# Summing the head scores of the odd tiles on TensorE, and spacing out GpSimd's products

## The chip, the cores and the metric

The kernel runs on one core of a Trainium2 chip. The metric is the device time of one execution in microseconds (us), and a version is judged by the median over its runs. A core has TensorE (PE in the profile, its weight loads PEld), VectorE (DVE), ScalarE (ACT) and GpSimd (POOL), and SyncE (SP), which here issues DMAs. They work side by side and wait for one another by semaphores. Each engine takes its own instructions strictly in the order in which they are written.

## The reference, cut to what matters

The reference is a stack of four blocks over 2 x 1024 tokens of width 128. Each block is a layer norm, an attention or mixing branch `s`, a gating feed-forward branch `g`, and `x = x + s * g`. The change touches the third one, whose attention runs over the 16 heads of one token and not over tokens:

```python
qkv = jnp.einsum('bnm,fm->bnf', x, Wqkv)          # 384 per token: q, k, v of 16 heads x 8
scores = jnp.einsum('bnhd,bngd->bnhg', q, k) / SCALE   # 16 x 16 per token, a sum over d = 8
attn = jax.nn.softmax(scores, axis=-1)
out = jnp.einsum('bnhg,bngd->bnhd', attn, v)
return jnp.einsum('bni,mi->bnm', out.reshape(b, n, -1), Wproj) + bproj
```

Beside it runs that block's feed-forward: 8 matrices, of which each position takes one, chosen by a position table.

## The kernel before

The 2048 tokens are cut into 16 tiles of 128. In the heads' attention a token lies on a partition, and one tile passes through these steps (generator `tile(i)`, one in each engine's program; the two tile buffers are taken in turn, `k = i % 2`):

1. TensorE projects the tile to q, k, v (`qkv`, a PSUM bank of 384 columns); ScalarE copies k and v to SBUF.
2. VectorE multiplies q by k for all pairs of heads: 16 x 16 x 8 = 2048 products per partition into `pr1[k]`. The sum index d, of length 8, runs innermost.
3. VectorE sums each 8 of them (`red(s, p1, ADD)`, 2048 read, 256 written into `sc2[k]`) and takes each head's negated maximum (`mx`, 256 read).
4. GpSimd adds the maximum (256 elements, "shifted"), ScalarE takes the exponential.
5. GpSimd multiplies with v in four instructions of 512 elements, the quarters, into `pr2[k]`; VectorE meanwhile sums the exponentials and takes the reciprocal.
6. VectorE sums the 2048 products of step 5 to 128 (`ot2[k]`, in the array `osb`), GpSimd scales them, TensorE turns the tile, ScalarE copies it out.

`pr1`, `pr2`, `sc2` and the q, k, v copies are pieces of one large SBUF array `ar`, so the profile names them all `ar`; `ps` is PSUM. Helpers record the instructions: L235 is every matmul, L238 a transpose by TensorE, L241 a tensor_tensor, L246 a tensor_scalar, L249 a scalar_tensor_tensor, L254 a reduce, L257 a copy, L278 an activation.

The program has three parts. `ORDER_A` and `ORDER_C` are tables: for each engine a string of step names, in which each name advances that step's generator by one `yield`. Between them stands the token attention of the first block, with steps woven in by slot (`LANES_B`). `ORDER_C` holds the second block's experts (`xturn`, `up`, `hturn`, `down` with numbers 2 and 3), its recurrence (`rec`), the heads' attention (`tile.0` to `tile.15`), the third block's feed-forward (`ffn2`: TensorE spreads a choice over a bank, VectorE multiplies it with the tokens into `psum_sb`, TensorE multiplies by the weights, eight times for each of four groups), the gathers of expert outputs (`gather`: GpSimd fetches rows to `gT` and `acc_sb`, VectorE adds them) and the fourth block. PSUM banks 4, 6 and 7 are handed out in turn in this part, and a matmul first waits until its bank has been emptied.

Of the kernel before, what the change touches and what calls it, by code (L numbers as in the profile page):

```python
# [37 lines left out]
for _name, _n in (("wqkvp", 512), ("wq", 128), ("wk", 128), ("wv", 128), ("bw", 128), ("cw", 128), ("wg1", 8),  # L38
# [45 lines left out]
    "vector": (  # L84
# [225 lines left out]

def rows_sem(q, i):
    return f"rows_in{i}" if q < 5 else f"last_rows_in{i}"


class Marks:

# [103 lines left out]
def _program(nc, A, out, ctx):  # L420
# [652 lines left out]
    def vector_program(dve):  # L1073
# [331 lines left out]
        def tile(i):  # L1405
# [18 lines left out]
            if i >= 2:  # L1424
                dve.wait_ge(*at(f"tile{k}_pool", i - 2, "av"))
# [1105 lines left out]
```

## Time and profile before

| what | value |
| --- | --- |
| median of 3 runs (lowest, highest) | 1131.12 us (1123.92, 1132.36) |
| the profiled execution | 1131.41 us, its span 1129.5 us |
| granted TensorE clock, mean over the span | 0.949 |
| busy PE / DVE / ACT / POOL | 1015.3 / 840.9 / 553.1 / 720.6 us |

The span runs from the first to the last instruction; 1.9 us of the execution lie around it. A busy share is an average over stages with different limits, so it is read by stretch below. Granted clock 1.00 is 2.4 GHz, and a stretch below 1.00 is a mix with time at 1.2 GHz. A TensorE matmul of 4-byte numbers appears as two records.

### The profile page before, as it was taken

To read this page: it belongs to the slowest core of one execution; us is meant where nothing else is said; L and a number is where in the kernel's file an instruction comes from. 1 tells how busy PE (TensorE), PEld (TensorE's weight loads), DVE (VectorE), ACT (ScalarE), POOL (GpSimd) and SP (SyncE) were. 2 spreads that over 40 slices of the span, in tenths; PEclk is the share of its full clock that TensorE was granted. 3 is DMA by queue.
4 is the path that set the end of the run, shared out by engine and by line. 5 is a ranking of instruction groups with operands and counts; after the bars stand their busy time and mean duration, and the time that the engine had idled before them with its cause. 6 is when DMAs were issued, how large, how long until landed. Compare 5 with 4: busy or idle time off the path is not lost.

```text
span 1129.5 us, 15337 instructions
## 1 busy us (share of the span) xinstructions
PE 1015.3 (90%) x4930; PEld 426.4 (38%) x4930; DVE 840.9 (74%) x1343; ACT 553.1 (49%) x911; POOL 720.6 (64%) x571
## 2 busy tenths in 40 slices
PE   5899989999999999999989986799957785789998
PEld 3356542222222222222212212567635322347675
DVE  6955768778788879787878525874799989997434
ACT  2564455656566665565556653443444111145353
POOL 5650527899987778997879993042476846861412
PEclk9999999999999999999999988899988786799999
DMA  9363612121111101212010112212200400101322
GB/s 325 102 197 99 181 49 69 29 60 30 33 39 36 35 14 48 60 58 63 20 32 23 37 29 64 90 62 75 80 10 19 182 15 19 47 24 39 97 65 71
DMA packets 84274, 74.19 MB, mean 66 GB/s; under 512 B 21612, under 2 KB 70124, under 8 KB 83300
## 3 DMA queue, kind: packets, MB, share of 16 engines
q1 hardware_dynamic: 70756, 62.45, 17.6%
q0 software_dynamic: 5120, 10.50, 3.2%
q10 hardware_dynamic: 8320, 0.26, 0.3%
q8 instruction: 42, 0.69, 0.3%
q14 instruction: 36, 0.29, 0.1%
HBM read 47.94 MB, written 24.77 MB: 64 GB/s over the span
## 4 chain that ended last, share of the span: by engine, by line
PE 62%; DVE 15%; POOL 11%; issue 4%; ACT 4%; ACTq 1%; DMA 1%; SPq 0%; POOLq 0%; DVEq 0%
PE ps L235 56%; POOL psum_sb L241 8%; PE ps L238 6%; DVE ar L241 4%; DVE ar L254 3%; ACT ar L278 2%; DVE small L254 2%; POOL xsort L295 1%; ACTq L281 1%; POOL ar L241 1%; DVE osb L254 1%; DMA psum_sb<-in_L_bv 1%; ACT lrow L275 1%; DVE ps L241 1%; DVE psum_sb L241 1%
## 5 line engine op out<-in xcount | busy, mean ns | idle before, releaser
L235 PE MATMUL ps<-ar 128*64 128x512 f32 (+3 forms) x2688 | 587.1, 484 | 17.4 <-ACT ar L278 5.8
L278 ACT ACTIVATE ar<-ps 128x1024 f32<-128x1024 f32 (+2 forms) x336 | 301.8, 902 | 194.0 <-PE ps L235 184.5
L254 DVE TENSOR_REDUCE small<-ps 128x2 f32<-128x1024 f32 (+2 forms) x276 | 312.6, 1146 | 64.7 <-PE ps L235 63.4
L235 PEld LDWEIGHTS ps<-ar 128*64 128x64 f32 (+2 forms) x2688 | 183.2, 135 | 383.0 <-issue 322.1
L241 POOL TENSOR_TENSOR psum_sb<-psum_sb,ar 128x1024 f32<-128x1024 f32 x128 | 308.0, 2407 | 22.6 <-ACT ar L278 7.6
L241 POOL TENSOR_TENSOR ar<-ar 128x512 f32<-128x512 f32 (+1 forms) x80 | 104.3, 1332 | 49.0 <-DVE ar L254 36.0
L300 POOL DMA_INDIRECT gT<-ysort,rt x48 | 46.3, 964 | 113.4 <-issue 113.0
L241 POOL TENSOR_TENSOR psum_sb<-ar 128x1024 f32<-128x1024 f32 x32 | 75.9, 2372 | 31.9 <-ACT ar L278 30.1
L275 ACT COPY ar<-ps 128x256 f32<-128x256 f32 (+2 forms) x84 | 33.8, 415 | 106.3 <-PE ps L238 55.8
L241 DVE TENSOR_TENSOR ar<-ps,ar 128x256 f32<-128x256 f32 (+4 forms) x56 | 56.4, 1010 | 34.2 <-PE ps L235 34.0
L241 DVE TENSOR_TENSOR on_sb<-osb,rec_sb 128x512 f32<-128x512 f32 x32 | 60.9, 1902 | 21.7 <-DMA rec_sb<-lscr 21.7
L235 PE MATMUL ps<-wA,xnT 128*128 128x512 f32 (+3 forms) x192 | 65.5, 454 | 11.8 <-DVE ar L241 6.0
L241 DVE TENSOR_TENSOR ar<-ar,ps 128x352 f32<-128x352 f32 (+1 forms) x88 | 50.3, 591 | 31.1 <-ACT ar L278 27.2
L235 PE MATMUL ps<-ar,onesf 128*32 128x512 f32 x256 | 62.9, 612 | 6.0 <-POOL psum_sb L241 6.0
L238 PE MATMUL ps<-cf,ar 128*128 128x128 f32 x368 | 56.7, 283 | 12.3 <-DVE ar L241 5.7
L295 POOL DMA_INDIRECT xsort<-ar,rt x32 | 32.2, 1005 | 43.9 <-DVE rt L257 36.5
L235 PEld LDWEIGHTS ps<-ar,psum_sb 128*128 128x128 f32 x464 | 56.1, 192 | 9.1 <-issue 8.3
L235 PE MATMUL ps<-ar,psum_sb 128*128 x464 | 58.8, 276 | 0.7 <-ACT ar L275 0.7
L238 PEld LDWEIGHTS ps<-cf,ar 128*128 128x128 f32 x368 | 45.5, 145 | 30.1 <-issue 16.4
L275 ACT COPY lrow<-ps 128x512 f32<-128x512 f32 x32 | 18.7, 585 | 64.6 <-PE ps L235 64.6
L254 DVE TENSOR_REDUCE ar<-ar 128x16 f32<-128x256 f32 (+1 forms) x48 | 49.6, 1033 | 0.6
L235 PE MATMUL ps<-ar,ps_sb 128*128 x96 | 48.5, 608 | 0.7 <-issue 0.6
(154 smaller groups left out, 1121.5 us busy)
## 6 DMA issues: line engine op xcount, KB each, us to landing
rec_sb<-lscr SPq DMA_DIRECT2D x64, 128.0 KB, 2.9
scr<-ar SPq DMA_DIRECT2D x48, 128.0 KB, 2.3
ar<-xsort SPq DMA_DIRECT2D x40, 128.0 KB, 2.3
ysort<-ar SPq DMA_DIRECT2D x40, 128.0 KB, 1.8
ar<-in_L_w SPq DMA_DIRECT2D x4, 1024.0 KB, 8.2
ar<-scr SPq DMA_DIRECT2D x32, 112.0 KB
xsort<-xs SPq DMA_DIRECT2D x12, 256.0 KB, 7.0
osb<-xsort SPq DMA_DIRECT2D x24, 128.0 KB, 2.5
```

Source lines behind the costliest of these rows:

```text
L235: return self.e.matmul(o, l, r, start=start, stop=stop) if self.e else Nothing()
L238: return self.e.transpose(o, i, idn) if self.e else Nothing()
L241: return self.e.tensor_tensor(o, a, b, op) if self.e else Nothing()
L254: return self.e.tensor_reduce(o, a, AX.X, op, negate=True) if negate else self.e.tensor_reduce(o, a, AX.X, op)
L275: return self.e.copy(o, a) if self.e else Nothing()
L278: return self.e.activation(o, a, fn, **kw) if self.e else Nothing()
L281: return self.e.dma_start(o, i) if self.e else Nothing()
L295: return self.e.indirect_dma_start(rows, bass.IndirectOffsetOnAxis(ap=index, axis=0), i, None)
L300: return self.e.indirect_dma_start(o, None, rows, bass.IndirectOffsetOnAxis(ap=index, axis=0))
```

## The change

For the eight odd tiles the sum over d moves to TensorE: eight matmuls with the identity as weights accumulate in one PSUM bank, each reading 256 products of one d, which lie 8 elements (32 bytes) apart. VectorE then reads the maximum and does the addition of step 4 out of that bank, in place of its sum and of GpSimd's addition. GpSimd's four quarters of step 5 are separated, in all 16 tiles: each but the last raises a semaphore, and the next waits for it. The tables `ORDER_A` and `ORDER_C` are new for every engine, except that GpSimd's string in `ORDER_A` and `LANES_B` stay. The steps in them are the same ones in another order, apart from one more step of each odd tile for TensorE and one less for GpSimd.

```diff
+PE_SUMMED = (1, 3, 5, 7, 9, 11, 13, 15)
...
@@ tensor_program, tile(i)
+            if i in PE_SUMMED:
+                b = take(ring[0])
+                pe.wait_ge(*vacant(b))
+                pe.wait_ge(*at("qk", i))
+                for d in range(8):
+                    ins = pe.mm(ps[:, b, 0:256], ident, pr1[k].rearrange("p (a d) -> p d a", d=8)[:, d, :],
+                                start=d == 0, stop=d == 7)
+                ins.then_inc(*filled(b, ("scores", i)))
+                yield
...
@@ vector_program, tile(i)
-                dve.wait_ge(*at(t, i - 2, "scores"))
+                dve.wait_ge(*(at("scores", i - 2) if i - 2 in PE_SUMMED else at(t, i - 2, "scores")))
...
+            if i in PE_SUMMED:
+                sp = ps[:, bank["scores", i], 0:256].rearrange("p (h g) -> p h g", g=16)
+                dve.wait_ge(*at("scores", i))
+                dve.red(mx, sp, ALU.max, negate=True).then_inc(*up((t, i, "max")))
+                dve.wait_ge(*at(t, i, "max"))
+                if i >= 2:
+                    dve.wait_ge(*at(f"tile{k}_pool", i - 2, "av"))
+                dve.tt(s3_, sp, mx.unsqueeze(2).to_broadcast([128, 16, 16]), ALU.add).then_inc(
+                    *emptied(("scores", i), (t, i, "shifted")))
...
@@ pool_program, tile(i)
-            pool.wait_ge(*at(f"tile{k}_dve", i, "max"))
-            pool.tt(s3_, s3_, mx.unsqueeze(2).to_broadcast([128, 16, 16]), ALU.add).then_inc(*up((t, i, "shifted")))
-            yield
+            if i not in PE_SUMMED:
+                pool.wait_ge(*at(f"tile{k}_dve", i, "max"))
+                pool.tt(s3_, s3_, mx.unsqueeze(2).to_broadcast([128, 16, 16]), ALU.add).then_inc(*up((t, i, "shifted")))
+                yield
...
             for h in range(0, 16, 4):
                 ins = pool.tt(o4[:, h:h + 4, :, :], s4[:, h:h + 4, :, :].to_broadcast([128, 4, 8, 16]),
                               v4.to_broadcast([128, 4, 8, 16]), ALU.mult)
-                if h == 4:
-                    yield
+                if h < 12:
+                    ins.then_inc(*up((t,)))
+                    if h == 4:
+                        yield
+                    pool.wait_ge(*last(t))
```

What the new tables do is seen in three places. The first is VectorE at tile 1. `ar<-ps,ar 128x2048` is the product of q and k, `ar<-ar 128x256` the sum over d, `ar<-ar 128x16` after it the maximum (and elsewhere the sum of the exponentials), `ar<-ar,ps 128x352` a product of the second block's experts. Before:

```order
L241 TENSOR_TENSOR ar<-ps,ar 128x2048
L249 SCALAR_TENSOR_TENSOR ar<-xnT,wA,ps 128x512
L254 TENSOR_REDUCE ar<-ar 128x256
L254 TENSOR_REDUCE ar<-ar 128x16
L241 TENSOR_TENSOR ar<-ar,ps 128x352 x2
L254 TENSOR_REDUCE ar<-ar 128x16
L260 RECIPROCAL ar<-ar 128x16
```

And of the changed kernel:

```order
L241 TENSOR_TENSOR ar<-ps,ar 128x2048
L241 TENSOR_TENSOR gT<-gT,acc_sb 128x512
L241 TENSOR_TENSOR ar<-ar,ps 128x352 x2
L254 TENSOR_REDUCE ar<-ar 128x16
L260 RECIPROCAL ar<-ar 128x16
L249 SCALAR_TENSOR_TENSOR ar<-xnT,wA,ps 128x512
L254 TENSOR_REDUCE ar<-ps 128x16
L241 TENSOR_TENSOR ar<-ps,ar 128x256
```

The sum over d is gone, six other instructions stand between the product and the maximum, and the maximum and the addition read `ps`.

The second is TensorE at the same tile. `ps<-wA,xnT 128x384` is the projection of tile 1, `ps<-cf,ar` are transposes, `ps<-ar 128x512` and `128x192` the experts. Before, from the projection on:

```order
L235 MATMUL ps<-wA,xnT 128x384 [waits bank7_empty]
L238 MATMUL ps<-cf,ar 128x128 [waits bank4_empty]
L238 MATMUL ps<-cf,ar 128x128 x2
L235 MATMUL ps<-ar 128x512 [waits rec_dve,bank6_empty]
L235 MATMUL ps<-ar 128x512
L287 TENSOR_LOAD rt [waits bank0_empty]
L235 ISA
```

And of the changed kernel, some rows behind the projection (`bank6_empty` in front of the sum is raised by VectorE's product):

```order
L235 ISA [waits bank2_empty]
L235 MATMUL ps<-ar 128x512
L235 ISA
L235 MATMUL ps<-ar 128x192
L235 MATMUL ps<-ar,cf 128x256 [waits bank6_empty]
L235 MATMUL ps<-ar,cf 128x256 x7
L238 MATMUL ps<-cf,ar 128x128 [waits bank7_empty]
L238 MATMUL ps<-cf,ar 128x128 x3
```

The eight matmuls of the sum stand among the experts' work, and the transposes of the next group of tokens are behind them.

The third is VectorE in the first group of `ffn2`, at the addition `gT<-gT,acc_sb` of the gathered rows. `osb<-ar 128x128` is step 6 of a tile, `psum_sb<-xnT,ps` a product of `ffn2`. Before:

```order
L254 TENSOR_REDUCE osb<-ar 128x128
L241 TENSOR_TENSOR psum_sb<-xnT,ps 128x512
L241 TENSOR_TENSOR gT<-gT,acc_sb 128x512
L249 SCALAR_TENSOR_TENSOR ar<-xnT,wA,ps 128x512
L254 TENSOR_REDUCE ar<-ar 128x16
```

And of the changed kernel:

```order
L254 TENSOR_REDUCE osb<-ar 128x128
L241 TENSOR_TENSOR psum_sb<-xnT,ps 128x512
L254 TENSOR_REDUCE ar<-ps 128x16
L241 TENSOR_TENSOR ar<-ps,ar 128x256
L241 TENSOR_TENSOR gT<-gT,acc_sb 128x512
```

The maximum and the addition of an odd tile, tile 7, stand just ahead of the addition of the gathered rows, which is otherwise where it was.

## Rows read from the trace of the kernel before

**Rows 1.** The page's busy times, and the chain that ended last by engine

```profile
PE 1015.3 (90%) x4930; PEld 426.4 (38%) x4930; DVE 840.9 (74%) x1343; ACT 553.1 (49%) x911; POOL 720.6 (64%) x571
...
PE 62%; DVE 15%; POOL 11%; issue 4%; ACT 4%; ACTq 1%; DMA 1%; SPq 0%; POOLq 0%; DVEq 0%
```

**Rows 2.** Stretches from 740 us: length, busy time by engine, granted clock, DMA, GB/s

```profile
740.00:828.00 88.00, 86.43 (x489) 63.55 (x488) 56.41 (x122) 41.45 (x104) 39.75 (x40) 1.00 0.23 68
828.00:889.00 61.00, 36.69 (x171) 24.88 (x170) 60.30 (x67) 22.50 (x41) 44.31 (x40) 0.85 0.15 49
889.00:937.00 48.00, 41.45 (x92) 14.73 (x93) 41.44 (x72) 7.67 (x14) 29.16 (x31) 0.76 0.22 78
937.00:1012.00 75.00, 53.30 (x162) 24.49 (x159) 72.71 (x104) 18.47 (x42) 53.57 (x50) 0.77 0.09 27
1012.00:1129.50 117.50, 111.56 (x616) 79.28 (x616) 62.66 (x127) 52.37 (x165) 32.13 (x34) 0.97 0.24 66
```

**Rows 3.** Groups by line and form, 828 to 1012 us: busy us, mean ns, idle before

```profile
L241 POOL TENSOR_TENSOR ar<-ar 128x512 f32<-128x512 f32 x56 | 82.4, 1502 | 11.4 <-ACT ar L278 10.5 <-DVE osb L254 1.0
...
L241 DVE TENSOR_TENSOR ar<-ps,ar 128x2048 f32<-128x2048 f32 x14 | 31.9, 2281 | 0.0
L254 DVE TENSOR_REDUCE ar<-ar 128x256 f32<-128x2048 f32 x14 | 31.8, 2269 | 0.0
...
L254 DVE TENSOR_REDUCE ar<-ar 128x16 f32<-128x256 f32 x27 | 11.2, 414 | 0.5
L241 POOL TENSOR_TENSOR ar<-ar 128x256 f32<-128x256 f32 x15 | 9.7, 649 | 24.4 <-DVE ar L254 24.4
```

**Rows 4.** One group, 750 us to the end: VectorE's 256-element operation out of PSUM

```profile
L241 DVE TENSOR_TENSOR ar<-ps,ar 128x256 f32<-128x256 f32 x20 | 8.3, 422 | 23.6 <-PE ps L235 23.6
```

**Rows 5.** TensorE's timeline, two places: start us, length us, records of one kind

```profile
891.95 2.08 PE L235 MATMUL ps<-psum_sb,on_sb 128*128 128x512 f32 x2
893.96 0.60 PE L235 MATMUL ps<-osb,ar 24*128 24x512 bf16 x1
...
1025.27 1.02 PE L235 MATMUL ps<-ps_sb,wA 128*128 128x512 f32 x2
1026.13 1.45 PE L235 MATMUL ps<-ar 128*128 128x256 f32 x4
1027.42 0.60 PE L238 MATMUL ps<-cf,acc_sb 128*128 128x128 f32 x4
1027.86 0.60 PE L238 MATMUL ps<-cf,ar 128*128 128x128 f32 x4
```

**Rows 6.** VectorE's line L241, 178 to 740 us: duration ns minimum/median/maximum

```profile
L241 DVE TENSOR_TENSOR small<-small,cf x2: 224/224/225, 731.5 to 734.3; 128x64 f32<-128x64 f32 x2
...
L241 DVE TENSOR_TENSOR small<-rt,small x2: 269/269/269, 732.8 to 735.3; 128x64 f32<-128x64 bf16 x2
```

**Rows 7.** Timeline of GpSimd and VectorE, and one piece of the chain (840.70)

```profile
840.67 5.78 POOL L241 TENSOR_TENSOR ar<-ar 128x512 f32<-128x512 f32 x4 [0.53 <-ACT ar L278]
840.70 5.84 DVE rec_sb L246 x4
...
899.57 5.79 POOL L241 TENSOR_TENSOR ar<-ar 128x512 f32<-128x512 f32 x4
900.08 5.83 DVE L241 TENSOR_TENSOR gT<-gT,acc_sb 128x512 f32<-128x512 f32 x1
...
929.40 0.68 DVE L241 TENSOR_TENSOR gT<-gT,acc_sb 128x512 f32<-128x512 f32 x1
...
931.19 1.11 DVE L246 TENSOR_SCALAR rec_sb<-xs,small 128x128 f32<-128x128 f32 x4
```

**Rows 8.** GpSimd's timeline where an instruction waits for its own forerunner

```profile
838.19 0.23 POOL L246 TENSOR_SCALAR small<-small 128x4 f32<-128x4 f32 x1 [0.87 <-DVE small L266]
838.50 1.05 POOL L241 TENSOR_TENSOR small<-small 128x4 f32<-128x4 f32 x1
```

**Rows 9.** Who waited for whom, 828 to 1012 us: us in total, times, longest

```profile
PE ps L235 <- DVE ar L241: 12.3, 6, 4.0
```

More of the change, by code:

```diff
@@ L1422, in tile @@
             yield
-            dve.wait_ge(*at("qk", i))
-            if i >= 2:
-                dve.wait_ge(*at(f"tile{k}_pool", i - 2, "av"))
-            dve.red(s, p1, ALU.add).then_inc(*up((t, i, "scores")))
-            dve.wait_ge(*at(t, i, "scores"))
-            dve.red(mx, s3_, ALU.max, negate=True).then_inc(*up((t, i, "max")))
+            if i in PE_SUMMED:
[7 more added lines that the diff above has]
+                    *emptied(("scores", i), (t, i, "shifted")))
+            else:
+                dve.wait_ge(*at("qk", i))
+                if i >= 2:
+                    dve.wait_ge(*at(f"tile{k}_pool", i - 2, "av"))
+                dve.red(s, p1, ALU.add).then_inc(*up((t, i, "scores")))
+                dve.wait_ge(*at(t, i, "scores"))
+                dve.red(mx, s3_, ALU.max, negate=True).then_inc(*up((t, i, "max")))
             yield
@@ L1819, in tile @@
             yield
-            act.wait_ge(*at(f"tile{k}_pool", i, "shifted"))
+            act.wait_ge(*at(f"tile{k}_dve" if i in PE_SUMMED else f"tile{k}_pool", i, "shifted"))
             act.af(sc2[k], sc2[k], ACT.Exp, scale=0.125).then_inc(*up(("tile_act", i, "exp")))
```

246 rows, old and new, of tables (ORDER_A, ORDER_C) are left out of this document.

## The prediction

> **What bounds the kernel now.** I read the page first for the busy times and for the chain that ended last: TensorE holds 62% of it, VectorE 15% [rows 1]. Those are averages, and the change sits in one part, so the second view is the table by stretches [rows 2]. From 740 to 828 us and from 1012 us to the end TensorE is busy 86.4 of 88.0 and 111.6 of 117.5 us: there a TensorE cycle is on the path. Between them it is the other way round. From 828 to 889 VectorE is busy 60.3 of 61.0 us and from 937 to 1012 it is busy 72.7 of 75.0, while TensorE has 36.7 and 53.3 at granted clocks of 0.85 and 0.77, so part of its time runs at 1.2 GHz. From 889 to 937 both have about 41.4 of 48: the feed-forward `ffn2` passes between them. In the 184 us from 828 to 1012 VectorE thus works 174.5 and TensorE 131.4, which leaves TensorE 52.6 us of idle time. Fourteen of the sixteen tiles have their product there [rows 3].
>
> **What leaves VectorE.** Each odd tile loses a sum over d of 2269 ns and gains an addition out of PSUM. The maximum stays (414 ns for 256 elements) and only changes its source [rows 3]. The addition is not in the trace; a 256-element tensor_tensor with one operand in PSUM takes 422 ns [rows 4], and I take that. So each tile saves 2.27 - 0.42 = 1.85 us. Of the eight odd tiles, tile 1 lies in the TensorE stretch before 828, where VectorE has room (56.4 of 88.0) and the saving is worth nothing. Seven tiles give 7 x 1.85 = **13.0 us**, on the engine that sets the end.
>
> **The gaps.** Twice VectorE stands still under GpSimd's quarters [rows 7]. At 900.08 the addition of gathered rows takes 5.83 us and ends as the four quarters (5.79 us) end; undisturbed it takes 0.68. At 840.7 four tensor_scalars take 5.84 us in place of 1.11, again as long as four quarters; but there they are four instructions for four quarters, so each got in at the border of one quarter. The single tensor_tensor did not get in at a border and waited for all four. A gap should let it in after at most one quarter, 1.50 us [rows 3], on average half of one: 5.83 - 0.68 - 0.75 = **4.4 us**, since the new order keeps that addition behind the same kind of work. For the tensor_scalars a gap changes little; whether they collide again depends on the new order, so 0 to 4.7 us, and I take **2.4**.
>
> What a gap costs: where GpSimd waits for its own forerunner the next one starts 0.08 us after the end (838.19 + 0.23 to 838.50) [rows 8]. 48 gaps are 3.8 us, against eight additions saved, 8 x 0.65 = 5.2 us [rows 3]. GpSimd is busy 127 of the 184 us [rows 2], so I put both at nothing; if GpSimd were the bound they would nearly cancel.
>
> **What lands on TensorE.** A sum is eight matmuls, so 16 records of 256 columns. At the full clock two records of 512 columns take 0.86 us (1025.27 to 1026.13), and 128-column records, each with a weight load of its own, follow at 0.11 us (four in 0.44), so loads are hidden and time goes with the columns [rows 5]. 16 records of 256 are then 16 x 0.215 = 3.4 us. At the lower clock two records of 512 take 2.01 us (891.95 to 893.96), which makes a sum about 7 us. Both hold for operands that lie in a row.
>
> These lie 32 bytes apart, and no TensorE row of the trace reads so. The nearest rows are VectorE's: a 64-element operation takes 269 ns where one operand is a slice with a step of 32 bytes (a choice out of the array of choices in `rt`), and 224 ns with plain operands [rows 6]. That is 0.7 ns for each strided read; the two also differ in type, so it is a hint. GpSimd's quarters, whose v is read at the same step, take 1502/512 = 2.9 ns an element against 649/256 = 2.5 for its plain addition [rows 3]. Both point to a surcharge short of a doubling. The bounds for one sum are 3.4 us (no surcharge, or less where a wait is filled) and 6.9 us (each read twice as dear, at the full clock); I take **5.0 us**.
>
> The Trainium skill says in "Advanced Engine Details and Errata", section Memory Cachelines, that SBUF lines are 16 bytes and a read is at full speed only if the following one hits the same line. At 32 bytes each read opens a new line. It gives no figure; it speaks for the upper bound, and the result by it is the second rival below.
>
> Where this lies: the sums of tiles 3 to 13 fall into the stretch in which TensorE has room. After VectorE gave up 13.0 + 4.4 + 2.4 = 19.8 us the room is 52.6 - 19.8 = 32.8 us, and 6.5 sums of 5.0 us fill 32.5 of it: just hidden. The sum of tile 1 stands among the experts of a stretch with TensorE 98% busy, and that of tile 15 behind the first matmuls of the last experts; they and half of a third are on the path, 1.5 x 5.0 = **7.5 us** back.
>
> **Clock.** In `ffn2` the pairs at 1.2 GHz are on the path now: 2.01 us where the same pair at the full clock takes 0.86, so about 1.1 us each, and with a clock of 0.76 about five of that stretch's pairs. If TensorE is busier ahead of them half of that comes back, **2.8 us**.
>
> **Latency and order.** The sum makes the way from product to exponential longer by 5.0 - 2.3 us, covered by the other tile's work, since six instructions now stand between on VectorE. For waits of TensorE's queue that the cover misses I set **1.5 us**. The tables of the first part move steps without changing work; at first order 0, bounds 4 us to either side.
>
> **Sum.** 13.0 + 4.4 + 2.4 + 2.8 = 22.6 us gained, 7.5 + 1.5 = 9.0 given back: -13.6 us. From the profiled execution, 1131.4 us (span 1129.5 and 1.9 around), that is 1117.8. The median of the runs is 0.3 below that execution. I predict **1118 us**, 1.2% less.
>
> **Rivals.**
>
> First, TensorE becomes the bound because its queue is in order. A sum must wait for VectorE's product, and everything behind it on TensorE waits too: the transposes of the next group, the experts' matmuls, `ffn2`'s spreads, and then VectorE waits for those. TensorE already waits for VectorE's work on `ar` 12.3 us in six waits, 2.05 us each, the longest 4.0 [rows 9]. If each sum brings such a wait and costs 6.9 us, 6.5 x 8.95 = 58 us meet a room of 32.8, 25 over; the sums in the full stretches add 1.5 x 8.95 = 13. That is 25 + 13 - 22.6 = +16 us: **1147**. It decides from 6.9 us for a sum s with its wait, where 6.5 s - 32.8 + 1.5 s reaches the 22.6 us gained. Against it speaks that a clock of 0.77 leaves TensorE work that gets shorter as it is kept busy.
>
> Second, each read costs double and nothing waits beyond that: 6.9 us a sum. Then 6.5 x 6.9 - 32.8 = 12 us over the room, 10.4 in the full stretches, and -22.6 + 12 + 10.4 = 0: **1131**, no change. The skill's section above would give this. The part of it that a faster clock hides pulls it down by up to 5 us.
>
> Third, the gain is not collected: what VectorE saves in `ffn2` and around it turns into waits for TensorE, because a third of the stretch passes between the two, and the four tensor_scalars or another operation collide again with quarters. Half of 13.0 and only the 4.4 remain, the 7.5 stay: -3.4, about **1128**.
>
> Fourth, more is gained: sums at 3.4 us, both collisions gone, the clock at its full rate: 13.0 + 9.1 + 5.6 - 5.1 = 22.6: **1108**.
>
> **How the numbers follow.** No change and a change of up to 1% cannot be told apart by this kernel's measurement; 1% of the median is 11.3 us, so faster begins below 1119.8. Chances: the forecast 0.45 (1112 to 1125, two thirds of it below 1119.8), more gain 0.13, doubled reads 0.17, not collected 0.13, TensorE as the bound 0.12. Faster is then 0.3 + 0.13 + 0.02 = 0.45, slower 0.12 + 0.01 = 0.13, the rest 0.42. The range leaves out the far half of the last case and the tip of the gain: 1107 to 1138.
>
> **What would show it.** The changed profile should have eight VectorE sums of 2.27 us less and eight 256-element additions near 0.42 more. TensorE's records of a sum start 0.22 us apart if the step is free, 0.43 at the full clock if it doubles them: this row decides between the forecast and the second rival. The stretch from the experts' end to the last product should be some 15 us shorter with a granted clock above 0.80. VectorE's addition to `gT` should nowhere take over 2.2 us. If it still takes four quarters, the gaps do nothing. The forecast is wrong if the first 740 us move by more than 4 us, or if TensorE's waits for `ar` grow.

## The result, and the profile after

The changed kernel takes **1168.5 us** (1166.7 to 1169.6), the kernel before 1131.1 beside it: a ratio of 1.034, 95% interval [1.030, 1.038]. It is slower by 3.4%; I had predicted 1118 us, with a range to 1138. The profiled execution has a span of 1166.7 us, 37.2 more than before.

Where these 37.2 us come from, by three landmarks: the first tile's product starts at 819.3 us (before 814.5), the last tile's reduction to `osb` starts at 1056.2 (before 1021.1), the end is at 1166.7. So 4.8 us are lost ahead of the tiles, 30.3 in the **stretch of the tiles** (first product to last reduction, 206.6 us before and 236.9 now), 2.1 behind. That stretch is the measure in all that follows. It is read from one profiled execution of each kernel. It doesn't hold the same work in the two orders: with the sums left out it has 550 of TensorE's records in the new order and 515 in the old one, so a comparison of the orders by it is rougher than one within an order.

The page's busy times, which answer to [rows 1]:

```profile
PE 1062.9 (91%) x5058; PEld 451.8 (39%) x5058; DVE 815.5 (70%) x1343; ACT 553.4 (47%) x911; POOL 717.3 (61%) x563
```

VectorE lost 25.4 us of work (15 of it in the tiles' sums), TensorE gained 47.6. The stretches, as in [rows 2] (length, busy time by engine, granted clock, DMA, GB/s), and the groups of the stretch of the tiles that answer to [rows 3] and [rows 4]:

```profile
740.00:828.00 88.00, 85.21 (x470) 61.31 (x469) 51.93 (x114) 38.59 (x94) 34.97 (x37) 1.00 0.25 71
828.00:889.00 61.00, 55.13 (x249) 34.46 (x248) 45.40 (x66) 21.86 (x45) 37.16 (x31) 0.99 0.07 19
889.00:937.00 48.00, 43.91 (x99) 15.95 (x99) 40.99 (x58) 7.58 (x14) 35.21 (x33) 0.86 0.29 108
937.00:1012.00 75.00, 52.21 (x133) 26.43 (x132) 56.42 (x111) 10.32 (x24) 44.14 (x43) 0.70 0.08 24
1012.00:1050.00 38.00, 37.77 (x134) 18.35 (x133) 23.48 (x40) 16.07 (x36) 18.28 (x16) 1.00 0.10 28
```

```profile
L235 PE MATMUL ps<-ar,cf 128*128 128x256 f32 x128 | 61.0, 645 | 3.1 <-DVE ar L241 3.1
...
L254 DVE TENSOR_REDUCE ar<-ar 128x256 f32<-128x2048 f32 x8 | 18.2, 2278 | 0.1
...
L241 DVE TENSOR_TENSOR ar<-ps,ar 128x256 f32<-128x256 f32 x11 | 4.7, 423 | 4.1 <-PE ps L235 3.8
...
L254 DVE TENSOR_REDUCE ar<-ps 128x16 f32<-128x256 f32 x8 | 3.4, 422 | 24.1 <-PE ps L235 24.1
```

VectorE did what I said: eight sums of 2.28 us are gone and the additions take 0.42. But it now waits 24.1 us for the sums, and no stretch of the table has it at over 86% of the time, where two had it at 97% and 99%. TensorE spends 61.0 us on the eight sums. Its timeline (start us, us, records of one kind), beside [rows 5]; the granted clock was 1.00 during the first two of these sums and 0.64 during the third:

```profile
827.98 7.53 PE L235 MATMUL ps<-ar,cf 128*128 128x256 f32 x16
...
849.39 7.62 PE L235 MATMUL ps<-ar,cf 128*128 128x256 f32 x16 [0.45 <-DVE ar L241]
...
954.50 7.60 PE L235 MATMUL ps<-ar,cf 128*128 128x256 f32 x16
```

A sum takes 7.5 to 7.8 us, 0.46 to 0.48 a record, hardly more at the low clock. And VectorE at the first of them, and its additions of gathered rows, which answer to [rows 7]:

```profile
835.55 0.42 DVE L254 TENSOR_REDUCE ar<-ps 128x16 f32<-128x256 f32 x1 [5.17 <-PE ps L235]
```

```profile
L241 DVE TENSOR_TENSOR gT<-gT,acc_sb x4: 681/682/682, 806.3 to 932.0; 128x512 f32<-128x512 f32 x4
```

The stall of 5.8 us is gone, and the four tensor_scalars (840.70 in [rows 7]) take 2.55 us in place of 5.84, since one of them still waits 1.59. TensorE's waits for VectorE's work on `ar` went from 12.3 us in six [rows 9] to 16.2 in ten, the longest 5.1 (over the stretch of the tiles, so a little wider).

### The profile page after: what moved, and what is told of

Its sections match the earlier page's. It is cut to its first block and busy times, and to the rows that moved or that the text cites. A ratio compares the mean times of both kernels' runs of the same rounds, so it can differ in the third digit from the quotient of the medians.

```text
span 1166.7 us, 15595 instructions
## 1 busy us (share of the span) xinstructions
PE 1062.9 (91%) x5058; PEld 451.8 (39%) x5058; DVE 815.5 (70%) x1343; ACT 553.4 (47%) x911; POOL 717.3 (61%) x563
## 5 line engine op out<-in xcount | busy, mean ns | idle before, releaser
L235 PE MATMUL ps<-ar 128*64 128x512 f32 (+4 forms) x2688 | 581.2, 481 | 21.0 <-ACT ar L278 7.5
L235 PEld LDWEIGHTS ps<-ar 128*64 128x64 f32 (+2 forms) x2688 | 179.4, 134 | 383.1 <-issue 325.1
L241 POOL TENSOR_TENSOR psum_sb<-psum_sb,ar 128x1024 f32<-128x1024 f32 x128 | 309.1, 2414 | 21.7 <-ACT ar L278 7.5
L241 POOL TENSOR_TENSOR ar<-ar 128x512 f32<-128x512 f32 (+1 forms) x72 | 101.7, 1415 | 72.2 <-ACT ar L278 36.7
L241 POOL TENSOR_TENSOR psum_sb<-ar 128x1024 f32<-128x1024 f32 x32 | 75.9, 2371 | 31.1 <-ACT ar L278 29.3
L241 DVE TENSOR_TENSOR ar<-ps,ar 128x256 f32<-128x256 f32 (+4 forms) x64 | 59.6, 938 | 40.9 <-PE ps L235 37.9
L241 DVE TENSOR_TENSOR ar<-ar,ps 128x352 f32<-128x352 f32 (+1 forms) x88 | 50.8, 591 | 39.5 <-ACT ar L278 32.0
L241 DVE TENSOR_TENSOR on_sb<-osb,rec_sb 128x512 f32<-128x512 f32 x32 | 56.6, 1770 | 21.9 <-DMA rec_sb<-lscr 21.9
L235 PE MATMUL ps<-ar,cf 128*128 128x256 f32 x128 | 61.0, 645 | 3.1 <-DVE ar L241 3.1
```

The source lines that it names most:

```text
L235: return self.e.matmul(o, l, r, start=start, stop=stop) if self.e else Nothing()
L241: return self.e.tensor_tensor(o, a, b, op) if self.e else Nothing()
```

## The experiments

The groups of runs fall on two levels. At the first one the kernel before takes 1131 us. At the second it takes 1191 to 1197 us: every kernel starts its token attention some 35 us later there and is 5 to 7 us longer behind the tiles. What sets the level is not shown; it isn't the chip's number, since runs on chip 7 stand at both. Ratios are always to the kernel before in the same group, and the stretch of the tiles is nearly the same at both levels: 199.0 and 199.2 us for the gaps alone, and within 2.2 us, 236.9 and 234.7, for the changed kernel. Direct times from different groups of the second level are compared below too; the kernel before differs by up to 6 us between these groups, so differences under that say little.

| kernel | ratio to before [95%] | stretch | PE busy in it | DVE busy |
| --- | --- | --- | --- | --- |
| before | 1 | 206.6 | 152.4 | 195.1 |
| old order, gaps | 0.994 [0.992, 0.996] | 199.0 | 149.8 | 190.7 |
| the same, second level | 0.994 [0.992, 0.996] | 199.2 | 149.2 | 190.5 |
| old order, gaps, VectorE relieved | 0.995 [0.992, 0.998] | 198.2 | 149.6 | 177.6 |
| new order, VectorE's own sums | 1.021 [1.019, 1.022] | 226.9 | 170.6 | 198.7 |
| new order, 1 matmul a sum, second level | 1.006 [1.003, 1.009] | 207.6 | 164.1 | 179.3 |
| new order, 4 matmuls a sum, second level | 1.010 [1.007, 1.014] | 208.7 | 177.0 | 178.7 |
| new order, 8 without a step | 1.011 [1.009, 1.012] | 210.0 | 172.1 | 178.6 |
| changed kernel | 1.034 [1.030, 1.038] | 236.9 | 203.6 | 178.8 |
| the same, second level | 1.027 [1.024, 1.031] | 234.7 | 201.9 | 178.7 |

### The parts of the change, each alone

**Without the step.** Each matmul of a sum reads 256 neighbours:

```diff
-pr1[k].rearrange("p (a d) -> p d a", d=8)[:, d, :]
+pr1[k][:, 256 * d:256 * d + 256]
```

> The changed kernel with one edit: each of the eight matmuls of a sum reads 256 products that lie in a row in place of 256 that lie 32 bytes apart. It leaves out the right choice of the products, so the scores of the odd tiles are not the reference's; sizes, waits and order are the same. In the changed kernel a sum's 16 records took 7.4 to 7.5 us. Theory A, the step sets the price on TensorE: a sum takes 3.4 to 3.8 us, eight of them save 30 us of TensorE, and since TensorE is 90% busy or more in most of the stretch, 20 to 30 us of the 37 lost come back: 1138 to 1148. Theory B, 16 short records with a weight load of their own each are the price: sums stay at 7 us and the time at 1166 to 1170. Theory C, the new order is at fault whatever a sum costs: sums shorten and the time stays above 1155.

Measured: 1143.7 us, 24.8 less than the changed kernel, its eight sums hold TensorE for 33.6 us in place of 61.0. The step of the reads alone is two thirds of the loss. The kernel is still 1.1% slower than before, so it isn't all.

**The order alone.** The new tables and the gaps, with VectorE doing the sum, the maximum and the addition of the odd tiles, and no matmuls:

> The new order of all engines and the gaps stay, but TensorE's sum is taken out and VectorE sums the products of the odd tiles as before; VectorE also does the 256-element addition. VectorE so carries 0.3 to 0.4 us a tile more than in the kernel before, 3 us in all, and TensorE nothing more. Theory A, TensorE's 60 us of sums are the loss: 1128 to 1140. Theory C, the order made for another set of durations costs time by itself: above 1145. What it comes out above the kernel before, less some 3 us for the additions and up to 5 us for the gaps, is the price of the order.

Measured: 1155.6 us, and a stretch of 226.9. The new order with the old work is 28 us longer than the old one with the gaps. It is an order made for a VectorE that has less to do, so this isn't yet its price in the change. Two things go into the 28 us beside the order: the profiled execution ran 4.8 us longer than the median, and TensorE was granted a clock of 0.77 in the stretch, in place of 0.82, at which its own work, without any sum, takes 170.6 us.

**The gaps alone**, in the kernel before:

> The kernel before, with its own order, and only the waits between GpSimd's quarters. In the changed kernel four quarters took 6.2 to 6.3 us in place of 5.8 to 5.9. The prediction's theory: the addition to gT no longer waits for four quarters, 4.4 us gained, and up to 2 us more or less from GpSimd's longer way: 1124 to 1130. Rival: VectorE does not get in at a gap either, or the 16 x 0.35 us of GpSimd land on the path: 1130 to 1136.

Measured: 1123.2 us against 1131.4, and the stretch 7.6 us shorter. The row of the addition, its longest 5832 ns before, and VectorE's four tensor_scalars, which took 5.84 us before:

```profile
L241 DVE TENSOR_TENSOR gT<-gT,acc_sb x4: 683/687/881, 797.3 to 919.9; 128x512 f32<-128x512 f32 x4
...
839.11 6.27 DVE L246 TENSOR_SCALAR rec_sb<-xs,small 128x128 f32<-128x128 f32 x4
```

So the gain comes from the addition alone; the tensor_scalars gain nothing. The addition is 4.95 us shorter, and the piece around it, from the eighth tile's product to the ninth's, is 8.7 us shorter. The rest is on TensorE: it waited 4.8 us behind the addition and now waits 0.2, and the same piece holds it busy for 32.0 us at a granted clock of 0.86 where it was 34.9 us at 0.81. The two pieces, before and with the gaps:

```profile
879.04:923.97 44.93, 34.95 (x81) 12.07 (x79) 39.33 (x62) 4.68 (x9) 32.14 (x33) 0.81 0.34 122
```

```profile
878.15:914.41 36.26, 32.02 (x78) 10.58 (x76) 34.17 (x62) 4.68 (x9) 31.09 (x31) 0.86 0.41 149
```

Four quarters take 6.25 us in place of 5.9 (median of the sixteen tiles), and that costs nothing that shows. This is the best version of the study that computes the reference; at the second level it gave the same:

> The gaps alone in the kernel before, once more, on the chip of the three runs beside it, since the last two groups of runs fell on a chip that loads its inputs later. From the first tile's product to the end it took 307.2 us where the kernel before took 315.0. If the gain of the gaps is one of the chip's, it is gone: a ratio of 1.000. If it is the gain of the gaps, 0.994 again.

Measured there: 0.994 again.

**The step moved to VectorE.** VectorE writes the odd tiles' products with d outermost, which makes it read k with the step along its innermost index, and TensorE reads neighbours:

> The changed kernel with the odd tiles' product written in another layout, d outermost: VectorE then reads q and k with the step of 32 bytes and writes in a row, and TensorE reads 256 in a row; the result is the reference's. Theory A1, the step costs only where it is read by TensorE: the product stays at 2.3 us, a sum takes 3.4 to 3.8 us, and the time is that of the run with contiguous reads. Theory A2, VectorE pays for the step too (0.7 ns for each of 2048 by the hint in the prediction, 1.4 us a product, or a doubling to 4.5 us): 5 to 15 us above that run.

Measured: 1153.4 us, 1.019. The sixteen products of VectorE (line, tile, busy us, mean ns) show the price:

```profile
L241 DVE TENSOR_TENSOR ar<-ps,ar 128x2048 f32<-128x2048 f32 x16 | 49.1, 3068 | 1.3 <-ACT ar L275 1.2
```

Half of them are as before, 2.28 us, so the others take 3.86. Who reads with the step pays for it, here 1.6 us on VectorE in place of some 3 us on TensorE (eight sums take 37.0 us here, 61.0 in the changed kernel).

**Without the gaps**, in the changed kernel:

> The changed kernel without the gaps between GpSimd's quarters. In the kernel before, the gaps alone gave 8 us back. If they are worth the same under the new order, this takes 1176. If the gaps cost in the new order (about 0.1 us for each of 48) and the collisions are gone with the order anyway, it takes 1164. The row that decides: the longest addition to gT, 5.8 us if it still waits for all four quarters.

Measured: 1231.7 us beside the changed kernel's 1228.9 at that level, the stretch 235.2 against 234.7, and the longest addition to `gT` 685 ns; one tensor_scalar waits 1.59 us, as it does with the gaps. In the new order no addition collides even without the gaps, so that they, worth 8 us in the old one, are worth nothing in the stretch and at most some 3 us in the median, which the spread of the runs doesn't settle.

**With the first table of before**, in the changed kernel:

> The changed kernel with the first table of the kernel before (all up to the token attention). The changed kernel began its token attention 2.5 us later and its first tile product 4.8 us later. If the first part of the order costs what it shows there, this takes 2 to 3 us less than the changed kernel, 1166. If the delay is taken up later anyway, it takes the same, 1168.

Measured: 1229.3 us beside 1228.9, each with a spread of 5 to 7 us. The time doesn't settle it. The traces do show a later start: at the first level the four kernels with the new first table start their attention at 164.3 to 164.7 us, the kernel before and the two there that keep its first table at 161.8 to 162.3; at the second the start varies more, 198.9 to 203.2 us with the new table and 194.1 to 198.8 with the old one. So the new first table costs 2.5 us or more at the attention; how much of that reaches the end is not shown.

### What a step costs TensorE

```diff
+step = {1: 1, 3: 2, 5: 4, 7: 8, 9: 2, 11: 4, 13: 1, 15: 8}[i]
-pr1[k].rearrange("p (a d) -> p d a", d=8)[:, d, :]
+pr1[k][:, 0:256 * step].rearrange("p (a e) -> p e a", e=step)[:, d % step, :]
```

> The changed kernel with another step for the elements of each sum: tiles 1 and 13 read neighbouring elements (step 4 bytes), 3 and 9 every second (8 bytes), 5 and 11 every fourth (16 bytes), 7 and 15 every eighth (32 bytes, as in the changed kernel). The scores of these tiles are not the reference's. It shows from which step a record of 256 columns leaves the 0.21 us it takes without one. If every step costs alike, the three strided ones take 0.46. If it goes by how many elements share a piece of memory that one access brings, 8 bytes cost less than 16, and 16 as much as 32 if a piece is 16 bytes.

TensorE's timeline, all eight sums in the order of the tiles, so with steps of 1, 2, 4, 8, 2, 4, 1 and 8 elements:

```profile
893.79 3.62 PE L235 MATMUL ps<-ar,cf 128*128 128x256 f32 x16
911.29 3.90 PE L235 MATMUL ps<-ar,cf 128*128 128x256 f32 x16 [0.45 <-DVE ar L241]
933.94 7.46 PE L235 MATMUL ps<-ar,cf 128*128 128x256 f32 x16 [0.20 <-DVE ar L241]
954.56 7.76 PE L235 MATMUL ps<-ar,cf 128*128 128x256 f32 x16 [1.67 <-DVE ar L241]
1013.06 6.23 PE L235 MATMUL ps<-ar,cf 128*128 128x256 f32 x16
1035.39 7.55 PE L235 MATMUL ps<-ar,cf 128*128 128x256 f32 x16
1057.79 6.09 PE L235 MATMUL ps<-ar,cf 128*128 128x256 f32 x16 [1.34 <-issue]
1086.06 7.53 PE L235 MATMUL ps<-ar,cf 128*128 128x256 f32 x16
```

At the full clock neighbours (the first) take 3.6 us and every second element (the second) 3.9; with the clock at 0.58 and 0.60 (the fifth and the seventh) they take 6.2 and 6.1. Every fourth and every eighth take 7.5 to 7.8 at granted clocks from 0.64 to 1.00. So 8 bytes are nearly free, 16 bytes cost as much as 32, and what is paid then hardly goes with TensorE's clock. It was one run of one kernel, but its sums at 32 bytes take what they take in the changed kernel.

The Trainium skill's rule of 16-byte lines ("Advanced Engine Details and Errata", section Memory Cachelines) fits the place where the price begins. The Trainium skill also asks there for at least two hits on a line: at 8 bytes two reads fall on each line, and from 16 bytes on each read has a line of its own. The trace agrees: 3.9 us beside 3.6, and then 7.5.

**No step anywhere.** ScalarE writes the odd tiles' k with d outermost, v is stored so, and VectorE's product and TensorE's sum read neighbours:

> The changed kernel with no stride left anywhere in the odd tiles: ScalarE writes k with d outermost (two copies in place of one), VectorE makes the product with d outermost from neighbouring elements, v is stored with d outermost too, TensorE sums neighbouring elements. The kernel with the product d-outermost out of a strided k took a ratio of 1.019 (its products 3.86 us), the one that read contiguously out of a false place 1.011. If the product is back at 2.28 us this takes 1.011 or a little less. If VectorE's product stays at 3.86 the cost is in its writing or its reading of q, and the ratio is 1.019.

Measured: products of 2.28 us again, the stretch 210.3 and 1211.5 us, 17.4 less than the changed kernel at that level. Since q is read here as in the run above, it was k's step that cost VectorE its 1.6 us. This kernel does the changed kernel's work without its step, with GpSimd 15 us lighter in the stretch besides, and is still slower than before: 1.018 [1.011, 1.025] to the kernel before, or 1.6% over the gaps alone (1192.7).

### Old order or new, and how many matmuls

**In the old order.** The tables of before with a word for TensorE's sum put in by hand where the product has just ended, and VectorE's maximum a few words later:

> The kernel before with its own tables, the gaps, and TensorE's sums for six of the eight odd tiles (1 to 11), each put by hand where VectorE's product has just ended; VectorE's maximum and addition stand a few instructions later than they did, and GpSimd's addition is gone for these six. Against the kernel with the gaps alone (1123). If the new order is the main loss and a sum by itself costs little, this takes about 1123 or less. If the sum is the loss wherever it stands (7.5 us in TensorE's queue, one of three PSUM banks held meanwhile), six sums cost up to 6 x (7.5 - 1.85) = 34 us where TensorE has no idle time, and about half of that here: 1135 to 1150.

> The same, with each matmul of a sum reading 256 products in a row (the wrong ones, so the scores of these six tiles are not the reference's; the work is the same). A sum is then 3.4 us. If the stride is what makes the sum dear, this takes 6 x 3.1 = 19 us less than the strided one at most, about 1120. If it is the place in the queue and the bank, both take the same.

Measured: 1229.6 us with the step and 1214.3 without, where the gaps alone take 1192.7. The first is a ratio of 1.039, more than the 1135 to 1150 us that I had expected. Six sums in the old order take as long as eight in the new one (1228.9), and their stretch is longer, 243.2 us, so the new order isn't what makes them dear. The 15.3 us between the two kernels are 2.6 for each sum. I placed these sums, and a better placing isn't ruled out: the first product to the end takes 357.2 and 338.0 us, 42 and 23 over the gaps alone.

Two sums, where TensorE waited for VectorE anyway:

> The kernel before with its own tables, the gaps, and TensorE's sums for tiles 3 and 5 alone, put where TensorE waited for VectorE in the kernel with the gaps (4.8 and 4.4 us of waiting). If a sum costs nothing where TensorE waits anyway, this gains 2 x 1.85 on VectorE over the gaps alone, a ratio to before of 0.991. If even there the sum is longer than the wait (7.5 us against 4.8 and 4.4) and puts off what stands behind it, up to 6 us are lost: a ratio of 0.999.

Measured: 1198.4 us, 6 more than the gaps alone, a ratio of 1.005 above both that I had expected, and a stretch of 206.7. TensorE's timeline at tile 3 shows a part of the reason (in this kernel the helpers stand two lines lower, so L237 is a matmul and L240 a transpose):

```profile
899.49 1.03 PE L240 MATMUL ps<-cb,small 128*24 128x128 bf16 x8 [5.44 <-DVE ar L243]
900.45 0.48 PE L240 MATMUL ps<-cf,osb 128*128 128x128 f32 x1
900.72 7.60 PE L237 MATMUL ps<-ar,cf 128*128 128x256 f32 x16
908.14 0.62 PE L240 MATMUL ps<-cf,rec_sb 128*128 128x128 f32 x4
```

Before the sum lies a wait of 5.4 us that the sum can't use, since it is the product of this very tile that TensorE's queue waits for; the sum then starts and the transposes of the next group, which had 4.8 us of waiting ahead of them, come 2.4 us later than without it, counted from the first product.

**Fewer matmuls in the new order.** `for d in range(4)` and `range(1)` in place of 8, with the changed kernel beside them:

> The changed kernel with four of the eight matmuls of every sum (d from 0 to 3; the odd tiles' scores leave out the other half). The stride is as in the changed kernel, a sum takes 3.8 us in place of 7.6, as long as the whole one did with neighbouring elements. If only the time that a sum holds TensorE counts, this lands where the contiguous one did, a ratio of 1.011. If reading with a stride also disturbs other work (SBUF reads of other engines), it stays above: 1.018 or more.

> The changed kernel with one matmul of the eight in every sum (d = 0 alone; the odd tiles' scores leave out the rest), so that TensorE gives 0.95 us to a tile and VectorE is relieved as in the changed kernel. This is the new order with next to none of the work that was moved. If the order is at fault, it stays above the kernel before: 1.005 to 1.02. If the sums' time on TensorE is at fault, the line through 61 us of sums (1.033) and 30 us (1.011) reaches at 8 us a ratio of 0.995, about the gaps' gain alone; if VectorE's relief is worth something once TensorE is free, less: 0.985.

> The changed kernel once more, for the same reason. A ratio of 1.033, and 347 us from the first tile's product to the end. If the chip that loads later also changes what follows, some 6 us more there.

Measured: 1203.7, 1202.7 and 1228.9 us. Stretch, TensorE busy, VectorE busy of the three (one, four, eight matmuls; each fence row is the stretch of the tiles of one kernel, in this order):

```profile
877.52:1085.15 207.63, 164.12 (x566) 82.26 (x567) 179.31 (x285) 63.10 (x131) 138.51 (x123) 0.84 0.14 46
```

```profile
883.63:1092.35 208.72, 176.97 (x614) 90.51 (x615) 178.67 (x285) 63.11 (x131) 138.38 (x123) 0.87 0.14 45
```

```profile
875.49:1110.14 234.65, 201.90 (x678) 103.43 (x679) 178.73 (x284) 63.00 (x131) 138.97 (x123) 0.90 0.12 40
```

The eight sums take 9.3, 31.5 and 61.0 us of TensorE. From one matmul to four TensorE works 12.9 us more and the stretch grows by 1.1; from four to eight it works 24.9 us more and the stretch grows by 25.9. There is room, and it has an end: with about 32 us of idle time left (31.8 and 32.8) TensorE takes no more. The clock makes a part of the room: the sums grew by 22.2 us in the first step and TensorE's busy time by 9.3 less than that, as the granted clock rose from 0.84 to 0.87 and its other work got shorter; in the second step 4.6 us came back so, at 0.90. Four with the step (3.9 us a sum) and eight without it land at the same ratio, so what counts is how long a sum holds TensorE, and reading with the step disturbs nobody else that shows.

The chain's shares over the stretch of the tiles say the same of the two ends, the old order with the gaps and then the changed kernel:

```profile
by line: PE ps L235 25.2%; DVE ar L241 14.7%; DVE ar L254 12.8%; issue 8.6%; POOL ar L241 8.2%; DVE osb L254 7.2%; PE ps L238 3.9%; DVE rec_sb L246 3.6%; DVE psum_sb L241 3.2%; DVE ps L241 1.7%; DVE ar L257 1.1%; DVE small L263 1.1%; DVE xs
```

```profile
by line: PE ps L235 62.1%; DVE ar L241 8.5%; issue 5.9%; PE ps L238 4.4%; DVE osb L254 4.0%; POOL ar L241 3.9%; DVE ar L254 2.6%; DVE psum_sb L241 1.5%; ACT ar L275 1.2%; DVE ps L241 1.0%; DVE small L263 0.6%; ACT ar L278 0.5%; DVE rec_sb L
```

### Is VectorE's time worth anything

**In the old order**, with the gaps:

```diff
-dve.red(s, p1, ALU.add)
+dve.red(s, p1[:, :, 0:1] if i % 2 else p1, ALU.add)
```

> The kernel before with its own tables and the gaps, where VectorE's sum over d of the odd tiles reads one product of each eight (256 elements in place of 2048; their scores leave out the rest). VectorE is relieved of 8 x 1.85 us, nothing is put on TensorE, nothing stands elsewhere. If VectorE sets the end of the stretch of the tiles in the old order, seven of the eight count: 13 us less than the gaps alone, a ratio of 0.983. If it does not (TensorE, GpSimd or the way through a tile sets it), the ratio stays near 0.994 and the stretch at 199 us.

Measured: 1124.5 us, a ratio of 0.995, where the gaps alone had 0.994. VectorE works 13.1 us less in the stretch, 177.6 us, and the stretch is 198.2 us, 0.8 less; TensorE's busy time and clock are the same. **Spread over the tiles, the relief is worth next to nothing.** That doesn't make all of VectorE's time worthless: the 4.95 us that the gaps took off one addition, with TensorE waiting behind it, came back in full. The relief turned into waits: VectorE's for GpSimd before its reductions to `osb` went from 1.1 to 3.2 us, those for TensorE before its copies grew too. A piece of the chain (start us, us, what) shows what then sets the pace, from a tile's quarters to the next exponential:

```profile
962.97 1.55 issue
964.51 1.12 POOL xsort L295
965.64 0.30 issue
965.94 0.96 POOL xsort L295
...
973.53 0.96 POOL xsort L295
...
974.51 0.64 POOL ar L241
975.17 0.43 ACT ar L278
975.60 0.07 issue
975.67 1.50 POOL ar L241
```

GpSimd issues eight indirect DMAs, 10 us, ahead of a tile's addition. But GpSimd alone isn't the bound either. With v stored so that its quarters read neighbours:

> The kernel before with the gaps, and v kept with d outermost (the columns of its weights are stored in that order), so that GpSimd's quarters read v in a row and not at 32 bytes. If the step costs GpSimd what its plain additions suggest (2.5 ns an element against 2.9), a quarter goes from 1.50 to 1.30 us and the 64 of them lose 13 us of GpSimd's time, of which perhaps a fifth is on the path: a ratio to before of 0.991. If GpSimd reads at one pace whatever the step, nothing changes against the gaps alone: 0.994.

Measured: a quarter takes 1268 ns in place of 1502, GpSimd works 14.6 us less, and 1192.3 us stand against 1192.7 of the gaps alone at that level; the stretch is 199.6. (Its ratio, 1.0005, comes with a kernel before that ran 4 us faster in that group; the two direct times and the two spans, 1189.5 and 1190.4, are the better comparison.) Both reliefs at once:

> The kernel before with the gaps, with VectorE relieved of 8 x 1.85 us (the odd tiles' sum over d reads one product of eight, so their scores leave out the rest) and GpSimd relieved of 64 x 0.23 us (v stored with d outermost). Each alone left the stretch of the tiles at 198 to 200 us. If the two engines take turns as the bound, so that a relief of one is taken by the other, both together shorten the stretch by 5 to 10 us: a ratio of 0.985 to 0.99. If TensorE and the order in which the four engines hand work on set it, it stays at 198 to 200 and 0.994.

Measured: 0.993 [0.990, 0.996], and a stretch of 198.6. With 12 us off VectorE and 14 off GpSimd the old order keeps its length within 1 us. The products of the tiles show where: the eighth starts 62 us after the first in place of 65, and the ninth 106 us in place of 101; between them lie the last experts' rows, their gathers and `ffn2`. The piece from the eighth to the ninth product, with the gaps alone and with both reliefs:

```profile
940.83:977.02 36.19, 31.24 (x79) 10.47 (x77) 33.91 (x61) 4.68 (x9) 31.21 (x31) 0.91 0.41 149
```

```profile
934.37:978.96 44.59, 38.94 (x79) 12.79 (x77) 34.35 (x61) 4.68 (x9) 31.00 (x33) 0.73 0.34 124
```

The same 79 records hold TensorE for 7.7 us more, at a granted clock of 0.73 in place of 0.91, and the piece is 8.4 us longer. In the rest of the stretch the two reliefs together save 9 us. So in this profiled execution the reliefs were worth something, and a lower clock of TensorE took it back. Why the clock fell there is not shown. The relief of VectorE alone lost nothing to the clock, and what took its 13 us beyond the waits named above stays open.

## Why the prediction was wrong, point by point

**"Seven tiles give 7 x 1.85 = 13.0 us, on the engine that sets the end": this step failed first.** I took VectorE's 98.9% and 97% busy in two stretches for the bound [rows 2]. With that work taken out and nothing else touched, the stretch in the old order got 0.8 us shorter and the median no shorter, where I had forecast 13.0. My reading is that an engine that is busy nearly all the time while its partners wait in turn is one of several that fit tightly. In the new order the same relief seems to count: from VectorE's own sums to one matmul a tile VectorE loses 19.4 us of work and the stretch 19.3 (some 16 us by the ratios). But TensorE's clock rose too, from 0.77 to 0.84, and what each of the two gave isn't told apart. And that order starts 28 us higher.

**Order, "at first order 0, bounds 4 us": failed.** The new order with one matmul a tile has a stretch of 207.6 us against 199.0 with the old one, though VectorE does 11 us less in it. That is 8.6 us, beside 4.8 us ahead of the tiles and 2.1 behind, together 15.5. The 8.6 hold more than the order: eight single matmuls, 9.3 us of TensorE, and the 35 records that the new order has inside the stretch and the old one outside of it.

**The sum, 5.0 us with bounds of 3.4 and 6.9: mis-sized.** It is 7.6, above my upper bound, because I had drawn it from a matmul's pace at one clock and a doubling. The row that was to decide, 0.22 or 0.43 us a record, shows 0.46. The hints that I took for a surcharge short of a doubling came from VectorE and GpSimd [rows 3, 6]; there the same step does stay short of it, 3.86 against 2.28 us on VectorE and 1.50 against 1.27 on GpSimd, and TensorE pays more. And the pairs of [rows 5] at the low clock, 2.01 us each, make 8.0 us for a sum of neighbours and not about 7; measured were 6.1 at a clock of 0.60.

**Room, "52.6 - 19.8 = 32.8 us, 6.5 sums just hidden": failed in its use.** The room is idle time less what can't be filled, and in the new order with four or eight strided matmuls a sum 32 to 33 us of the stretch stayed idle (31.8, 32.8 and 33.3). Of 61 us of sums the first half was hidden (1.1 us), and of the second half 28.2 us weren't (208.7 to 236.9; 25.9 with both at the second level).

**The gaps, 4.4 + 2.4 = 6.8 us and no cost: the sum came near by luck** for the old order, 7.6 in the stretch and 8 in the median. The addition gave 4.95 us, near the forecast 4.4; the tensor_scalars gave nothing (6.27 against 5.84 us), and TensorE's shorter time at a higher clock, which was no part of this term, made up for it. A gap cost 0.12 us and not 0.08, by the medians 5.88 and 6.25 us of four quarters. In the changed kernel the gaps add nothing, since no addition collides there even without them.

**The clock, 2.8 us:** it rose in the two stretches up to 937 us to 0.99 and 0.86 and fell behind them to 0.70, where I had asked for over 0.80. Against the kernel before, what it gave back isn't told apart. Within the new order it is: 9.3 + 4.6 us of TensorE's time, from one matmul a sum to eight. Little of it reached the end, since the second step cost 25.9 us all the same.

Together the stretch, read from kernel to kernel: -7.6 for the gaps (or for an order without collisions), +8.6 for the order with VectorE relieved and one matmul a sum, +1.1 and +28.2 for the matmuls, which is the 30.3 measured; with 4.8 and 2.1 around it the 37.2 of the span.

Of the rivals the first had half of the mechanism, TensorE as the bound through long sums, and gave 1147. The waits that it put in front of the sums, 2.05 us each, were not there: 3.1 us in all eight. It lacked the order's 15 us and took 6.9 for 7.6. The second had the size of the sum nearly right and 1131, because it believed in the 22.6 us gained too. The third had the fate of VectorE's time, which turns into waits, but at half of its size, and left the sums at 7.5 us. Every case that I priced began with all or half of VectorE's gain and with no cost of the order, and so none reached 1168.

## What to carry to other kernels

Busy at 98% is no proof of a bound in an order whose engines fit closely; take the work out of that engine alone, leave all else, and see if the end moves, before anything is moved elsewhere. Look at TensorE's granted clock in each piece while doing so, since it can hide a gain: here 8.4 us of it. Of another engine's idle time only part is room: here 12 of 44 us were filled almost free, and beyond that each microsecond counted nearly in full, so a move that is small in work still has to be small in time. And where an operand is read with a step, price the reads before the move: in this kernel, for steps of 16 bytes and more on TensorE, 2.1 times the time of neighbours at the full clock and 1.25 times at a clock of 0.60; at 32 bytes 1.7 times on VectorE and 1.2 on GpSimd.

## What the runs showed of the hardware

- TensorE with 4-byte operands, 256 columns a record: 0.23 us for neighbours at the full clock and 0.38 at 0.60 of it, 0.24 at a step of 8 bytes, 0.47 at 16 and at 32 bytes at granted clocks from 0.64 to 1.00. Eight records at 32 bytes took 4.06 us at a clock of 0.50 and 3.84 to 3.93 at 1.00.
- VectorE's product of 2048 elements: 2.28 us, and 3.86 where k is read at 32 bytes along the innermost index. GpSimd's product of 512: 1.50 us with v at 32 bytes, 1.27 without.
- A VectorE addition of two SBUF operands waited 5.83 us for four GpSimd products that followed each other directly [rows 7], and never over 2.4 us in the kernels with a wait on a semaphore between them. Four VectorE tensor_scalars beside four such products took one product's time each with the waits (6.27 us) and without (5.84). Such a wait costs 0.12 us (5.88 to 6.25 us for four products with three of them, medians).
- TensorE's same 79 records took 31.2 us at a mean granted clock of 0.91 and 38.9 at 0.73.
